# A graph attention kernel of three edge layers: two message quarters earlier on VectorE, and the block product moved to the end of TensorE's round

## The reference, cut to what matters

```python
def gat_conv(x, src, dst, W, att_src, att_dst, bias, n_nodes):
    h = (x @ W).reshape(n_nodes, Hh, Cc)
    a_src = (h * att_src).sum(-1)
    a_dst = (h * att_dst).sum(-1)
    alpha = leaky_relu(a_src[src] + a_dst[dst])
    m = jax.ops.segment_max(alpha, dst, num_segments=n_nodes)
    e = jnp.exp(alpha - m[dst])
    denom = jax.ops.segment_sum(e, dst, num_segments=n_nodes)
    w = e / jnp.clip(denom, 1e-16)[dst]
    out = jax.ops.segment_sum(w[:, :, None] * h[src], dst, num_segments=n_nodes)
    return out.reshape(n_nodes, Hh * Cc) + bias
...
x = _layernorm(x + _L0_gnn_ref(x, edge_index, ...))
x = _layernorm(x + _L1_gnn_ref(x, src, dst, ...))
```

## Time and profile before

| what | value |
|---|---|
| median of 3 runs | 6530.64 us (6526.72 to 6537.1) |
| the profiled execution's own time | 6552.36 us |
| its span, first to last instruction | 6550.3 us |
| TensorE matmul busy | 4781.3 us, 73% |
| VectorE busy | 4564.3 us, 70% |
| GpSimd busy | 4532.0 us, 69% |
| ScalarE busy | 2734.9 us, 42% |
| mean granted TensorE clock | 0.838 of full |

### The profile page before, as it was taken

One profiled execution on the slowest core, in us unless ns is written; L12 is line 12 of the kernel. 1 busy time (PEld: TensorE's weight loads), 2 busy tenths in 40 slices (PEclk: granted clock), 3 DMA queues, 4 the chain that ended last, 5 costly groups with the idle time before them and its releaser, 6 DMA issues. The chain is left out here.

```text
span 6550.3 us, 105533 instructions
## 1 busy us (share of the span) xinstructions
PE 4781.3 (73%) x21848; PEld 3433.9 (52%) x21849; DVE 4564.3 (70%) x13234; ACT 2734.9 (42%) x4932; POOL 4532.0 (69%) x4736
## 2 busy tenths in 40 slices
PE   6777777777777577777777777765776777677776
PEld 5555555555555455555555555544555555555555
DVE  6666666666666667777777777766766776677676
ACT  3343444344344334444444444433444444444443
POOL 2777777777777477767777777737777777777774
PEclk8788888888878778878887888877998999989898
DMA  8555555555555355555555555535555555555553
GB/s 271 146 149 150 148 152 147 149 149 149 148 148 150 99 150 163 162 155 159 160 159 158 162 159 159 162 105 150 158 156 152 153 156 156 149 156 154 153 154 97
DMA packets 477595, 1000.76 MB, mean 153 GB/s; under 512 B 143755, under 2 KB 284975, under 8 KB 476654
## 3 DMA queue, kind: packets, MB, share of 16 engines
q0 software_dynamic: 226208, 633.50, 36.6%
q1 hardware_dynamic: 250574, 356.73, 17.1%
HBM read 918.52 MB, written 71.30 MB: 151 GB/s over the span
## 5 line engine op out<-in xcount | busy, mean ns | idle before, releaser
L867 POOL DMA_INDIRECT e_rows<-table,loaded x4689 | 4513.6, 963 | 1883.7 <-issue 1670.9
L1160 PE MATMUL e_p_mm<-e_rows,e_onehot 128*128 128x264 f32 x9378 | 2762.9, 445 | 139.3 <-DVE e_rows L1354 109.2
L1160 PEld LDWEIGHTS e_p_mm<-e_rows,e_onehot 128*128 128x128 f32 x9378 | 1973.5, 219 | 555.4 <-issue 203.7
L1354 DVE TENSOR_TENSOR e_rows<-e_rows,e_p_pair 128x1024 f32<-128x1024 f32 x1173 | 1413.6, 1205 | 0.0
L1622 DVE TENSOR_TENSOR_SCAN e_fwd<-e_mask,e_p_one 64x128 f32<-64x128 bf16 (+1 forms) x294 | 121.9, 415 | 1294.4 <-PE e_p_one L1250 1294.4
L1346 DVE TENSOR_TENSOR e_onehot<-e_col,e_p_pair 128x512 f32<-128x512 f32 (+1 forms) x1176 | 903.1, 768 | 79.3 <-issue 76.1
L1250 PE MATMUL e_p_one<-ident,e_srcc 128*64 128x128 f32 (+1 forms) x294 | 91.2, 310 | 1006.9 <-issue 644.4
L997 ACT ACTIVATE e_onehotT<-e_onehotT,minus_pidx 128x2432 bf16<-128x2432 bf16 x294 | 680.8, 2316 | 21.2 <-DMA e_pass<-pass_rows 21.2
L1000 ACT ACTIVATE e_onehotT<-e_onehotT,one_col 128x2432 bf16<-128x2432 bf16 x294 | 682.6, 2322 | 9.6
L1250 PEld LDWEIGHTS e_p_one<-ident,e_srcc 128*64 128x64 f32 (+1 forms) x294 | 36.8, 125 | 1120.1 <-issue 1120.1
L1152 PE MATMUL e_p_mm<-e_rows,e_onehot 128*128 x1764 | 469.5, 402 | 208.9 <-DVE e_rows L1354 207.7
(11 more groups left out here) (323 smaller groups left out, 5384.7 us busy)
## 6 DMA issues: line engine op xcount, KB each, us to landing
e_onehotT<-rel_rows SPq DMA_DIRECT2D x294, 608.0 KB
e_rows<-table,loaded POOLq DMA_INDIRECT x4689
e_own_row<-table SPq DMA_DIRECT2D x196, 128.0 KB, 3.2
table<-e_rows_out SPq DMA_DIRECT2D x98, 132.0 KB, 2.7
table<-n_rows_out SPq DMA_DIRECT2D x14, 910.0 KB, 13.8
table<-e_rows_out SPq DMA_DIRECT2D x98, 130.0 KB, 3.0
n_inputs<-in_x_turned SPq DMA_DIRECT2D x14, 896.0 KB, 10.7
e_mask<-mask_rows SPq DMA_DIRECT2D x196, 64.0 KB
```

The source lines that it names most:

```text
L867: pool.indirect_dma_start(rows[k][:, g, 0:TW], None, table[L], bass.IndirectOffsetOnAxis(ap=idx[k][:, g:g + 1], axis=0)).then_inc(s_gat[k] ...
L1160: ins = nc.tensor.matmul(p_mm[:, bass.ds(region, MW)], onehot[:, g, :], rows[k][:, g, :], start=False, stop=True, skip_group_check=True)
L1354: return nc.vector.tensor_tensor(feats, feats, p_e[:, gs, :].unsqueeze(3).to_broadcast([P, n, H, C]), ALU.mult)
```

## The change

On VectorE the third quarter goes ahead of `adst` and the columns, and the fourth goes ahead of the logits. On TensorE `extras` and `products(3)` go ahead of `fmat`; `turn` and then `multiply` close the round, and `multiply` takes the block turned in the same round, one younger than before. In the first round behind a jump the scores are turned before the four loads of offsets (in the third layer `last_sums` too). On ScalarE `take_turned` goes behind `factor`. What runs past the last window is shifted to match.

```diff
@@ ScalarE, body
-                    if CARRY and finished(w, 6):
-                        take_turned(w, u)
                     act.wait_ge(st["fmat"], now)
                     wait(act, st["rescaled"], past)
                     nc.scalar.activation(factor[:], p_small[:, MAT_AT:MAT_AT + H], ACT.Exp).then_inc(st["factor"], 1)
+                    if CARRY and finished(w, 6):
+                        take_turned(w, u)
@@ TensorE, multiply
-                    r = (u - 7) % TURNS
-                    wait_apart(pe, s["xT"], place_of(pe, w, 7))
-                    if finished(w, 8):
-                        wait_apart(pe, s["row"], place_of(pe, w, 8))
+                    r = (u - 6) % TURNS
+                    wait_apart(pe, s["xT"], place_of(pe, w, 6))
+                    if finished(w, 7):
+                        wait_apart(pe, s["row"], place_of(pe, w, 7))
@@ TensorE, body
+                    behind_jump = u == 0 and not isinstance(w, int)
+                    if not behind_jump:
+                        regions, offs, flag, extra_ad, slots = round_words()
...
-                    if CARRY and finished(w, 7):
-                        multiply(w, u)
+                    if behind_jump:
+                        regions, offs, flag, extra_ad, slots = round_words()
...
+                    products(2)
+                    if not first:
+                        extras((k - 1) % BUFS, words(pe, WINDOW_ROW, (w - 1) * WIN + W_TILE, EXTRAS, G - 1), past)
+                    products(3)
+                    wait_apart(pe, st["fdist"], now)
+                    nc.tensor.matmul(p_small[:, MAT_AT:MAT_AT + H], first_row[:], fdiff[:], start=True, stop=True
+                                     ).then_inc(st["fmat"], 1)
                     if CARRY and finished(w, 6):
                         wait_apart(pe, st["topread"], now)
                         turn(w, u)
-                    products(2)
-                    if not first:
-                        old_slots = words(pe, WINDOW_ROW, (w - 1) * WIN + W_TILE, EXTRAS, G - 1)
-                    wait_apart(pe, st["fdist"], now)
-                    nc.tensor.matmul(p_small[:, MAT_AT:MAT_AT + H], first_row[:], fdiff[:], start=True, stop=True
-                                     ).then_inc(st["fmat"], 1)
-                    if not first:
-                        extras((k - 1) % BUFS, old_slots, past)
-                    products(3)
+                        multiply(w, u)
@@ TensorE, past the last window
+                if CARRY:
+                    multiply(WINDOWS, WINDOWS % UNROLL)
+                for w in range(WINDOWS + 1, BLOCKS + 7) if CARRY else ():
+                    turn(w, w % UNROLL)
                     multiply(w, w % UNROLL)
-                    if finished(w, 6):
-                        turn(w, w % UNROLL)
@@ VectorE, body
                     quarters(1)
+                    quarters(2)
                     dve.wait_ge(st["carry"], now)
...
-                    quarters(2)
+                    quarters(3)
                     dve.wait_ge(st["adst"], now)
...
-                    quarters(3)
                     if CARRY:
                         carried(w, u, i)
```

More of the change, by code:

```diff
@@ L1238, in body, with round_words @@
                     now, past = ago(0), ago(1)
-                    if not first:
[L1240 to L1243, removed]
+                    def round_words():
+                        regions = None if first else words(pe, REGION_ROW, (w - 1) * G, G, (REGIONS - 1) * BANK)
+                        offs = words(pe, AD_ROW, w * G, G, (PLACES - 1) * ADS_W)
+                        flag, *extra_ad = words(pe, WINDOW_ROW, w * WIN + W_FLAG, 1 + EXTRAS, (PLACES - 1) * ADS_W)
+                        slots = words(pe, WINDOW_ROW, w * WIN + W_TILE, EXTRAS, G - 1)
+                        return regions, offs, flag, extra_ad, slots
+                    behind_jump = u == 0 and not isinstance(w, int)
+                    if not behind_jump:
+                        regions, offs, flag, extra_ad, slots = round_words()
                     def products(q):
@@ L1297, in _ @@
                     pe.wait_ge(st["topread"], W0 + WINDOWS)
-                    multiply(WINDOWS, WINDOWS % UNROLL)
                     turn(WINDOWS, WINDOWS % UNROLL)
@@ L1311, in _ @@
                     pe.sem_inc(s_mm[q], 1)
-                for w in range(WINDOWS + 1, BLOCKS + 8) if CARRY else ():
+                if CARRY:
+                    multiply(WINDOWS, WINDOWS % UNROLL)
+                for w in range(WINDOWS + 1, BLOCKS + 7) if CARRY else ():
+                    turn(w, w % UNROLL)
                     multiply(w, w % UNROLL)
-                    if finished(w, 6):
-                        turn(w, w % UNROLL)
                 if LINEAR:
```

## The result

The changed kernel takes **6851.6 us** (median of 4 runs, 6849.1 to 6854.0) against 6528.9 us before (4 runs), a ratio of 1.0493 (95% interval 1.0477 to 1.051). It is slower by 323 us, where 469 us were forecast against the same median (7000 less 6531), and inside the range. The profiled execution took 6853.0 us with a span of 6850.7 us, 300.4 us more than the span of the earlier trace rows.

A forecast was written before the change was run, and what follows sets the result against it. Bound by order and waits: the gathers, and TensorE's sequencer in the first two layers. Layers one and two +252 and +238, written-out rounds +34, layer three -51: +473 us on 6531, rounded to 7000 us; range 6690 to 7130 us.

The forecast's parts named there:

- The mechanism: TensorE, first two layers: offset loads, before beside extras and products(3), now stand behind the wait for xT, uncovered; chance 0.64.
- loads do not wait: TensorE: the sequencer passes the multiply's wait, loads run beside products; about 19 us a round, 6330 us; chance 0.08.
- only the visible idle moves: TensorE: loads take 2.6 us, starting when the matmuls are through; 21.7 us a round, 6590 us; chance 0.13.
- Short loads: TensorE: loads cost 2.4 us from the wait for xT; 20.5 us a round, 6490 to 6531 us; chance 0.06.
- Stream: TensorE round, layers one and two: from the scores through the last product, turn and fmat included, 17.0 us.
- Clock: TensorE, layers one and two: the clock rises later, so products(1) runs longer; 0.65 us a round, bounds 0 and 1.5.
- Wait for `xT`: TensorE, end of the round: the multiply waits 0.77 us for ScalarE's two copies behind the turn.
- "0.3" of issue and "5.2" of loads: TensorE, behind the wait for xT: issuing three matmuls takes 0.3 us, then the four offset loads 5.2 us.
- The jump: Loop jump, layers one and two: costs 3.8 and 4.3 us of its own; reordering there gains 1.4 us a turn.
- The written-out rounds: Rounds outside the loop, seven per layer with a multiply: about 22.9 us against 20.5, +34 us in all.
- Layer three: No multiply or turn there: GpSimd's waits behind jumps go, the gathers bind; 122.8 us a turn, -51 us.
- The clock's rival: TensorE: the clock stays low through products(1), a round 0.85 us longer than forecast; 7140 us; chance 0.09.

## Why the prediction was right, and where its size was off

**The mechanism held.** The loads stand behind the wait for `xT`, uncovered. Making the wait early (the turn early), taking the loads from behind it (ahead of `fmat`) or taking the multiply from the end gives back 440, 335 and 498 us. The rival "loads do not wait" falls with the changed kernel itself, and "only the visible idle moves" with the 5.02 us between L1222 and the scores. "Short loads" falls too: the Trainium skill (DMA: Bandwidth & Descriptors, section "Latency and other measured facts") has 600 ns as a floor for one load, and the merged load saved 0.25 us while every word costs 0.07 to 0.09; the floor does not tell what a load of many words takes, here the measurement does.

**The round was 23.8 us in the forecast and 22.8 measured** (22.80 and 22.85, the 70 rounds of each layer that don't start behind a jump). By its terms:

- Stream: "17.0 us, turn and fmat included". Measured 17.0 in layer one (L1230 starts at 16.56 and takes 0.44), 17.15 in layer two.
- Clock, "0.65 us": **mis-sized.** products(1) takes 2.43 and 2.54 us on average, and took 2.17 and 2.19 before, so the clock costs 0.26 and 0.35 us. I set one row of 2.34 against one of 2.99, and both kernels have rounds of either kind. Less still comes on top of the 17.0, which were read from a round with products(1) at 2.34 already: 0.1 and 0.2 us.
- Wait for `xT`, "0.77": right, 0.77 us in the row above. L1222 starts at 17.9 and 17.8 us (the 56 rounds neither behind nor ahead of a jump), where the forecast, clock included, has 18.4.
- "0.3" of issue and "5.2" of loads, 5.5 us: **mis-sized**, 4.90 and 5.08 us measured. The 5.2 came from taking 0.85 us of issue off a 6.05 us gap; no run tells issue and loads apart there, so which of the two was off is open.
- Sum: 0.5 us too much up to L1222 and 0.6 behind it in layer one, 0.6 and 0.4 in layer two: 23.9 less 1.1 or 1.0.

**The jump** was forecast to add 2.4 us to six ordinary rounds in layer one (3.8 of its own less 1.4) and 2.9 in layer two (4.3 less 1.4). It adds 3.4 and 3.0 us: five rounds of 22.8 and one of 26.2 or 25.8 us. Its own cost can be read against the end of the written-out rounds of layer one, where neither loads nor a jump stand between the multiply and the scores:

```profile
401.12 1.13 PE L1222 MATMUL e_p_node<-e_wmat,e_turned_x 128*128 128x264 f32 x4 [0.96 <-ACT e_turned_x L1047]
402.08 0.28 PE L1223 MATMUL e_p_node<-e_bias_parts,e_sum_parts 65*128 65x264 bf16 x1
402.20 0.27 PE L1257 MATMUL e_p_one<-ident,e_srcc 128*64 128x128 f32 x1
```

That is 1.1 us where a gap that ends at a jump has 4.5 and 4.3, so the jump itself takes 3.4 and 3.2 us, less than the 3.8 and 4.3. But the reordering gained less than 1.4. L1266 comes 4.8 and 4.7 us behind the scores in place of 1.45, so 3.3 us of the loads are in the open behind a jump, against 3.8 us (4.9 less 1.1) in an ordinary round: some 0.5 us gained. I had left out that loads put behind the scores no longer run beside the multiply. In layer one the turn comes out: 145.2 less 6 x 1.0 plus 1.0 is 140.2 us, and 140.3 is measured. In layer two the two misses cancel, which is luck.

**The written-out rounds** were to lose 34 us: the first twelve lost 0.5 and 1.9 us, round 96 another 3.1 and 2.0. Rounds 7 to 10 are 1.5 to 1.9 us longer, but rounds 1 to 6, without a turn, run 20.0 us where 20.5 stood, and round 11 ends ahead of the loop, where the loads stand behind the scores. I had given the early quarters nothing there, in the third layer neither, where these rounds gained 6 us.

**Layer three** was 122.8 us a turn in the forecast and is 122.9: GpSimd's waits for TensorE fell from 59.1 to 34.8 us in 12 turns, and the gathers bind. At the jump whose scores start at 5169.19 GpSimd goes on without a stop:

```profile
5168.44 0.95 POOL L867 DMA_INDIRECT e_rows<-table,loaded  x1 [0.30 <-issue]
5169.69 0.95 POOL L867 DMA_INDIRECT e_rows<-table,loaded  x1 [0.30 <-issue]
```

`extras` waits nowhere. The clock's rival, products(1) at 3.9 us, did not come; the longest is 3.1 us.

One sum of the forecast is wrong as it stands: with "short loads" and no clock term the round of 20.5 us is 0.3 us shorter than before, which makes -50 - 40 - 51 = -141 us and not 0. The rival had a chance of 0.06, so little hangs on it.

So the total, beside the forecast's +473: the rounds of the loop -84 and -80 us, the jump +14 in layer one and +1 in layer two, the written-out rounds -27 and -6. The kernel before took 127.0 and 128.3 us a turn over all 14 turns, not the 127.2 and 128.7 of rows 4, which is +9, and layer three gained 48 us and not 51, +3. That is +303, beside 300 in the spans.

## What to carry to other kernels

On TensorE here, register loads ran beside the queued matmuls only as long as the last wait ahead of them was met early. Before putting work at the end of a round, look at when its input is ready: an operation whose input is made just above it (turn, copy, multiply) holds all that the sequencer does behind it (here 4.9 us from L1222 to the scores), while one whose input is a few microseconds old costs little more than its own time (2.35 us from L1222 to the scores with the turn early). And an idle gap called issue is a remainder: the work behind it is as long as the gap plus what covers it.

## What was not expected of the hardware

On TensorE a register load costs 0.07 to 0.09 us a word, and each load some time besides: 0.25 us by merging two, 0.5 to 0.7 us by adding one (the table above). In the change the words are the larger part.

On the two other chips every kernel loses 7 to 13 us a round at the same place: VectorE's reduction behind the lookups waits for a signal long after the last lookup has run. TensorE and VectorE, kernel with the early quarters but without the jump's part, first round of the first layer, timelines:

```profile
165.97 0.17 PE L1168 MATMUL e_p_one<-ad_parts,e_onehotT 128*128 x1 [2.60 <-issue]
167.38 0.17 PE L1168 MATMUL e_p_one<-ad_parts,e_onehotT 128*128 x1 [1.24 <-issue]
168.78 0.17 PE L1168 MATMUL e_p_one<-ad_parts,e_onehotT 128*128 x1 [1.23 <-issue]
```

```profile
193.96 0.36 DVE L1670 TENSOR_REDUCE e_adst<-e_p_one 128x64 f32<-128x192 f32 x1 [31.14 <-remote]
```

The signal comes 25 us behind the last lookup, and SyncE's transfer that waits for the same signal starts at 194.04. The first chip, with the multiply at the front, has its three lookups there in one row, 0.55 us behind the others, and VectorE starts 0.03 us behind the end of the last:

```profile
165.08 0.51 PE L1168 MATMUL e_p_one<-ad_parts,e_onehotT 128*128 x3 [0.55 <-issue]
```

```profile
165.62 0.36 DVE L1670 TENSOR_REDUCE e_adst<-e_p_one 128x64 f32<-128x192 f32 x1 [1.72 <-PE e_p_one L1168]
```

What delays the signal there was not found. It changes what an order is worth: with the turn at the end of the round the three-load kernels take 0.92 of the kernel before on these chips, with the turn in the middle and four loads it is 0.975, and where the multiply stands hardly matters (0.9196 and 0.9216). The changed kernel itself did not run there. But the kernels with three loads and with five of 50 words are the changed kernel in all else and take 0.92 and 0.93 of the kernel before, so by them the change, 4.9% slower on the first chip, would be 7 to 8% faster on these (an estimate). A verdict on an order of work holds for the chip it was measured on.
